# One request for the second tile of x, x laid out by tiles, and ten warm-up products in a two-layer kernel on TensorE

## The reference

```python
selected_W = W[cat_ids]
x = x + einsum('bsd,bdh->bsh', x, selected_W) + selected_b[:, None, :]
h = relu(einsum('bsd,bdf->bsf', x, wi[type_label]))
eo = einsum('bsf,bfd->bsd', h, wo[type_label])
s0, s1 = relu(x @ swi[0]) @ swo[0], relu(x @ swi[1]) @ swo[1]
gate_in = concatenate([eo[:, 0], s0[:, 0], s1[:, 0]], axis=-1)
w = softmax(relu(gate_in @ g1) @ g2, axis=-1)
x = x + eo * w[:, 0] + s0 * w[:, 1] + s1 * w[:, 2]
```

## Time and profile before

| | |
|---|---|
| median of 3 runs | 268.65 us (268.18 to 268.87) |
| the profiled execution, its own time | 268.71 us |
| its span, first to last instruction | 266.8 us |
| PE busy | 262.8 us, 99% of the span |
| DVE, ACT, POOL busy | 162.8, 150.0, 162.2 us |
| read and written in HBM | 16.00 and 2.10 MB |

### The profile page before, as it was taken

The page is one execution under the profiler, slowest core; times in us unless marked ns, Lnnn a source line. Parts: engine busy times, 40 slices in busy tenths (PEclk is TensorE's granted clock), DMA queues, the critical chain, the costliest instruction groups (busy, mean ns, idle before and its releaser), DMA issues.

```text
span 266.8 us, 3464 instructions
## 1 busy us (share of the span) xinstructions
PE 262.8 (99%) x1162; PEld 218.5 (82%) x1162; DVE 162.8 (61%) x246; ACT 150.0 (56%) x267; POOL 162.2 (61%) x171
## 2 busy tenths in 40 slices
PE   8999999999999999999999999999999999999995
PEld 8888888888888888888888888888888888888884
DVE  4679968635645434654445575345476577985664
ACT  3586457866575555665655644646545755645320
POOL 0269999999958949938944725625626528535000
PEclk9999999999999999999999999999999999999999
DMA  5654322012022012202022012012022022000404
GB/s 181 195 175 160 118 79 80 18 64 80 7 74 79 12 68 79 60 22 79 0 79 81 21 57 81 8 72 80 2 79 79 0 81 77 2 0 0 160 1 157
DMA packets 7473, 18.31 MB, mean 69 GB/s; under 512 B 1312, under 2 KB 2080, under 8 KB 7456
## 3 DMA queue, kind: packets, MB, share of 16 engines
q1 hardware_dynamic: 6880, 17.18, 19.4%
q10 hardware_dynamic: 576, 0.92, 1.0%
HBM read 16.00 MB, written 2.10 MB: 68 GB/s over the span
## 4 chain that ended last, share of the span: by engine, by line
PE 99%; DVE 0%; issue 0%; DVEq 0%
PE acc L755 48%; PE chain L755 23%; PE right L755 12%; PE left L755 6%; PE acc L764 4%; PE left L944 2%; PE left L810 1%; PE corner L755 1%; PE right L810 1%; PE corner L810 1%; PE chain L810 1%; DVE x L746 0%; DVE ones L641 0%; DVEq L745 0%
## 5 line engine op out<-in xcount | busy, mean ns | idle before, releaser
L296 POOL TENSOR_TENSOR m_lo<-staged,m_hi 128x512 fp32r<-128x512 f32 (+2 forms) x49 | 82.9, 1703 | 76.7 <-ACT m_hi L378 62.7
L755 PE MATMUL acc<-h_hi,m_hi 128*128 128x512 f32 x190 | 73.9, 389 | 0.0
L755 PE MATMUL acc<-h_lo,m_hi 128*128 128x512 f32 x190 | 73.9, 389 | 0.0
L755 PE MATMUL acc<-h_hi,m_lo 128*128 128x512 f32 x190 | 73.9, 389 | 0.0
L402 ACT COPY kept<-chain 128x512 f32<-128x512 f32 x66 | 38.9, 589 | 53.5 <-PE chain L755 53.5
L755 PEld LDWEIGHTS acc<-h_hi,m_lo 128*128 128x128 f32 x190 | 35.7, 188 | 7.4
L755 PEld LDWEIGHTS acc<-h_lo,m_hi 128*128 128x128 f32 x190 | 35.7, 188 | 7.4
L755 PEld LDWEIGHTS acc<-h_hi,m_hi 128*128 128x128 f32 x190 | 35.7, 188 | 7.3
L534 DVE SCALAR_TENSOR_TENSOR h_lo<-left,h_hi 128x512 fp32r<-128x512 f32 x24 | 16.6, 691 | 28.5 <-ACT h_hi L414 28.5
L296 POOL TENSOR_TENSOR staged<-staged 128x128 f32<-128x128 f32 x66 | 31.0, 484 | 1.7
L539 DVE TENSOR_TENSOR left<-left,kept 128x512 f32<-128x512 f32 x22 | 15.3, 695 | 23.9 <-PE left L755 23.9
(11 more groups left out here) (151 smaller groups left out, 441.7 us busy)
## 6 DMA issues: line engine op xcount, KB each, us to landing
staged<-mlp_w SPq DMA_DIRECT2D x22, 512.0 KB, 3.3
x<-x_t SPq DMA_DIRECT2D x5, 256.0 KB, 5.1
staged<-mlp_w SPq DMA_DIRECT2D x4, 256.0 KB, 3.3
out_t<-x SPq DMA_DIRECT2D x2, 512.0 KB, 3.3
x<-x_t ACTq DMA_DIRECT2D x3, 256.0 KB, 3.4
g_sb<-g SPq DMA_DIRECT2D x1, 768.0 KB, 3.8
out_t<-x SPq DMA_DIRECT2D x3, 256.0 KB, 2.3
w_raw<-cat_w SPq DMA_DIRECT2D x4, 128.0 KB, 2.3
```

What stands on the lines that cost most here:

```text
L296: return nc.gpsimd.tensor_tensor(out, a, b, ALU.subtract)
L755: last = nc.tensor.matmul(out[:, columns], half[:, slot, at:at + P], moving[:, columns], start=(start and n == 0), stop=(stop and n == 2), ...
```

## The change

Three things are changed. On the host, x is laid out by tiles: for each partition first both halves d of tile 0 (4 KB in one piece), then both halves of tile 1. The second tile of the first batch element is fetched by a single request of 128 rows of 4 KB, issued by ACT, in place of one request by SP and one by ACT; ACT issues it once `w_requested` is raised, in place of once part (0,0,0) has landed, and the semaphore `tile_loaded` stands for both parts. The second group of warm-up products has six in place of seven, so there are ten.

```diff
-WARMUP = (4, 7)
+WARMUP = (4, 6)
...
+        tile_loaded = sem("tile_loaded")
...
         def load_x(eng, b, t, d):
-            eng.dma_start(x1_part(b, t, d), x_t[b][:, d, t * TOK:(t + 1) * TOK]).then_inc(x_loaded[b][t][d], 16)
+            eng.dma_start(x1_part(b, t, d), x_t[b][:, t, d, :]).then_inc(x_loaded[b][t][d], 16)
...
-                if b == 0:
-
-                    load_x(sp, 0, 1, 0)
                 sp.dma_start(bias[:, b, :], cat_b[bass.ds(cat, 1)].rearrange("a p d -> p (a d)")).then_inc(bias_loaded[b], 16)
...
-                        sp.wait_ge(x_loaded[0][1][DC - 1], 16)
+                        sp.wait_ge(tile_loaded, 16)
...
             def x_hi_of(b, t, d):
-                act.wait_ge(x_loaded[b][t][d], 16)
+                act.wait_ge(tile_loaded if (b, t) == (0, 1) else x_loaded[b][t][d], 16)
...
-            act.wait_ge(x_loaded[0][0][0], 16)
-            load_x(act, 0, 1, 1)
+            act.wait_ge(w_requested, 1)
+            act.dma_start(x1[:, 0, 1, :, :], x_t[0][:, 1, :, :]).then_inc(tile_loaded, 16)
...
-        "x_t": np.asarray(x).reshape(B, S, DC, P).transpose(0, 3, 2, 1),
+        "x_t": np.asarray(x).reshape(B, S // TOK, TOK, DC, P).transpose(0, 4, 1, 3, 2),
```

More of the change, by code:

```diff
@@ L47, in build @@
 def build(nc, x_t, cat_w, cat_b, mlp_w, ids, g1, g2, out_t):
-    B, _, _, S = x_t.shape
+    B, _, HALVES, _, _ = x_t.shape
     D = DC * P
-    HALVES = S // TOK
     BANKS = mlp_w.shape[0]
```

## The result

The changed kernel takes 269.75 us (median of 8 runs, 269.27 to 270.70) against 268.39 us (8 runs, 268.18 to 268.87): a ratio of 1.0046, 95% interval 1.0036 to 1.0057. By the ratio it is slower by 1.2 us (the medians differ by 1.4), where 0.2 us less was forecast, and it lies above the forecast range of 268.0 to 269.1. The profiled execution took 269.88 us with a span of 268.0, so 1.2 us more than the profiled one of before, and it can be accounted for in full.

What follows compares the result with a forecast made beforehand. PE, busy 99% of the span, was taken as the bound. Span 266.8 less 0.2 for the warm-up product, plus 1.9 around the span, less 0.06 for the median, gave 268.45 us; range 268.0 to 269.1.

Steps and rivals of the forecast that it cites:

- What bounds the kernel: Whole span: PE, busy for 99% of it, bounds the kernel and never stands still after 1.06 us.
- One warm-up product less, -0.2 us: Before layer 0: PE starts 0.43 us earlier, less 0.20 for one more product at half speed; 0.2 us gain taken.
- When the request goes out, 3.1 us: ACT's request of the second tile: issued at 3.1 us, once ACT's table activation ends at 3.13.
- The price of the overlap, 0.1 us with a bound of 1.2: Weights' first half beside the tile's transfer: 0.1 us of delay, lower bound 0, upper bound 1.2 us.
- The prediction's own sign of being wrong: Weights in the changed profile: the prediction is wrong if they land over 1 us late.
- The tile's landing, 7.6 us: Second tile of x: lands at about 7.6 us, bounds 6.4 and 8.4; costs nothing at 7.6, 0.2 us at 8.4.
- The layout, 0: Fetching parts of x in 2 KB rows at another stride: 0 us, either way.
- C: Rival, weights over 0.1 us late: 0.4 us of delay gives 268.6 us, the 1.2 us bound 269.35; chance 0.16.
- E: Slower rival, PE idles before its first real product and full speed comes later: 270.0 to 271.4 us; chance 0.10.
- F: Faster rival, array's full speed comes ahead of the first real product: 1.0 us won, 267.65 us; chance 0.06.
- the clock's moment: PE's array early in layer 0: goes from half to full speed at 7.24 us, the same moment as before.

Runs made afterwards that it cites:

- e2: The kernel before with six in place of seven warm-up products in the second group and nothing else: 268.61 us, ratio 1.0008.
- e3: The changed kernel with ACT's tile request held until SP has issued both halves of the weights: 268.50 us, ratio 1.0003.
- e4: The changed kernel with ACT's single tile request gated as before, by the landing of part (0,0,0): 268.90 us, ratio 1.0006.
- e7: The changed kernel with the tile's single request issued by SP, behind the weights in SP's own queue: 268.70 us, ratio 1.0006.
- e1: The kernel before with x laid out by tiles and nothing else changed: 268.72 us, ratio 1.0004.
- e6: The changed kernel with seven warm-up products in the second group again: 269.56 us, ratio 1.0037.
- e14: e10 with seven warm-up products in the second group: 269.08 us, ratio 1.0020.
- e8: The kernel before, old layout, with the second tile in one early request by ACT (256 rows of 2 KB, gated by `w_requested`): 268.59 us, ratio 1.0001.
- e13: e8 with six in place of seven warm-up products in the second group: 268.46 us, ratio 0.9996.
- e9: The changed kernel with the tile requested at once behind the first tile, without the wait for `w_requested`, ahead of both weight halves: 270.66 us, ratio 1.0071.
- e11: e3 with the first tile, too, in one request of 4 KB rows: 270.37 us, ratio 1.0063.
- e12: e3 with four warm-up products in the second group: 268.62 us, ratio 1.0012.
- e5: The changed kernel with the tile in two requests of 2 KB rows, both by ACT at the same early gate: 269.06 us, ratio 1.0018.
- e10: The changed kernel with each row of x in memory padded by 64 elements, so the tile's request has 256 rows of 2 KB: 269.10 us, ratio 1.0016.

## Why the prediction was wrong

**What bounds the kernel.** Right, but not read to its end. PE never waited before, yet an operand was nearly late: the second tile's cast ended at 8.27 + 0.62 = 8.89 for a load at 9.06. e2 shows what follows: PE may come earlier only until it stands before the tile.

**One warm-up product less, -0.2 us.** The start did come 0.39 us earlier in e2, but the gain is nil, since the tile's landing takes it back. The slack of 0.17 us at that place stood in the rows. In e2, e3, e4 and e7 the 24 products end 3.7 us after the tile's first cast starts (8.47, 8.06, 8.90 and 8.26, against 12.18, 11.77, 12.61 and 11.96). With its cast at 8.27 the kernel before could end them at 11.98 at best, an estimate from these traces: 0.2 us were to be won there, whatever the warm-up and the clock do.

**When the request goes out, 3.1 us.** Wrong: 2.82. ACT issued it as soon as `w_requested` was raised, while the table was being loaded. The 0.3 us put it ahead of the weights' second half, requested at 2.98; behind it, at 3.41 and 3.40, it cost nothing (e3, e7).

**The price of the overlap, 0.1 us with a bound of 1.2.** This is the step that failed. I priced the first half of the weights alone, since it gates the first product, and gave the second half no line of its own, for it had 1.8 us and more to spare. Its cast started 3.1 us later (8.46, against 5.37 in the trace of before), PE waited 0.76 us for it, and product 7 began 1.08 us late. That is nearly the whole 1.19; the rest is a slower pair behind the gap. e3, with the order of the two requests turned round, shows it: no loss. The prediction's own sign of being wrong, weights over 1 us late, came true for the half that it hadn't priced. The first half, too, was cast 0.75 us later in this trace (5.70 against 4.95), but that isn't shown to be the tile's doing: it was 0.42 and 0.62 us late in e1 and e4 (5.37 and 5.57), where the tile is requested only behind both halves.

**The tile's landing, 7.6 us.** It landed at 8.1, near the bound of 8.4. Asked for earlier, it wasn't there much earlier: 8.06 in e3 with a request at 3.41. It scatters, too: in e6, with the changed kernel's requests, it was there at 7.6.

**The layout, 0.** Right by itself (e1). Together with the early request it isn't: 4 KB rows cost 1.0037 (e6), padded 2 KB rows 1.0020 (e14, of which 0.3 us, 0.0011, lies at the end of the kernel), rows of the old layout 1.0001 and 0.9996 (e8, e13).

**The rivals.** C had the right mechanism for the wrong half, and a size too small: 1.2 us at most, against 3.1. The Trainium skill (DMA: Bandwidth & Descriptors, Queues, rings and completion order) lets the engines take turns between the queues, a packet at a time. The trace agrees from 6.0 to 7.0 us, where both queues move; from 5.25 to 5.75 us q1 moved 2 packets beside q10's 32, and whether it had work then no row shows. E did not come in the changed kernel, in whose profile the distances double up to some 7.2 us as before; it is seen in the profiles of e9, e11 and e12.

F's condition, the rise ahead of the first real product, did come in e7, e13 and e14, though not its gain. By the distances of the matmuls PE was at full speed from 4.2 us on in e13's profile, 5.2 in e7's, 5.7 in e14's, 6.7 in those of e2 and e4, 7.0 in e6's and 7.2 in the two that the prediction is about, with the first matmul at 1.06 in all of them. In e13 it came in the warm-up, six of whose matmuls then fit into 0.83 us:

```profile
4.23 0.83 PE L942 MATMUL left<-ones 128*128 128x128 f32 x6
5.33 0.69 PE L762 MATMUL acc<-x_hi,w_hi 128*128 128x512 f32 x2 [0.27 <-ACT w_hi L431]
...
7.52 0.70 PE L762 MATMUL acc<-x_hi,w_hi 128*128 128x512 f32 x2 [0.59 <-ACT w_hi L388]
```

What the clock gives, PE then spends waiting: 0.59 us for the second half here, 0.42 us for the tile in e7. F's 1.0 us was not to be had as long as the tile lands near 8. The sum had the clock's moment as a fixed 7.2; that it matched in the changed kernel's profile is luck.

**How late may the second half be?** In five profiles (e13, e14, e5, e6, the changed kernel) the cast of the second half starts at 6.97, 7.14, 7.59, 7.93 and 8.46, and the 24 products end at 11.87, 12.04, 12.48, 12.85 and 13.36, each 4.9 us later. Before, they ended at 12.17. So by these traces a cast that starts up to about 7.3 costs nothing, and each microsecond beyond costs a whole one. (In e10's profile the first half, cast at 7.17, decides; e9 and e11 lose their time ahead of the second half, by the first half and by the index.)

What stays open: how the queues hold the second half back. The times show that a tile requested ahead of it in one request of 4 KB rows costs about 1 us or more (the changed kernel, e6, e9), and in one request of 2 KB rows about nothing in layer 0 (e8, e13, e14); yet in two requests of 2 KB rows, one ahead and one behind, it costs 0.5 us (e5). The experiments show that it is so and not where the data queue up. Each landing time is from one profiled execution, and these scatter: in the changed kernel's own trace the first half came 0.75 us later than before, in e6's with the same requests 0.3 us.

## What to carry to other kernels

When a large transfer is moved ahead, list everything issued within the next microsecond behind it, on either queue, and give each its own time of need; the one with the most slack is the one that is forgotten. Before costing an earlier start of the bounding engine, find the next operand it would run into: here it had 0.17 us to win, whatever the warm-up. And a small read on which a request depends (an index) is a transfer like the others: look at its time too when large transfers are moved. Before a single trace is read as the effect of a change, see where its full speed began: that moved by 3 us between the kernels' profiles here.

## What the runs showed of the hardware

- A request by ACT went out at 2.82 us, 0.02 us after the semaphore that it waits for was raised, while ACT's table was still being loaded (1.64 to 2.92): the table load and the activation that stand before it in the program did not hold it.
- With 512 KB in rows of 4 KB requested 0.16 us ahead on the other queue, 128 KB took 5.46 us from request to landing, in place of 2.4 to 2.6. With the same bytes in rows of 2 KB it took 3.95 us (e13).
- A read of an index took 1.71 us in place of 0.51 when the first tile was asked for in one request of 4 KB rows (e11), and 1.96 in place of 0.85 in one execution with rows of 2 KB (e8).
- Full speed came anywhere from 4.2 to 7.2 us in profiles in which PE didn't stop for more than 0.4 us before it. With stops of 1.0 to 1.3 us before it, it came at 9.4 to 10.3 us (e9, e11, e12), with one of 0.8 us at some 8.1 (e8), but after a stop of 1.5 us it was there at once (e10). In the changed kernel it came before the stop of 0.76 us and stayed. The Trainium skill (TensorE: Matmul & The Clock Gate, Part 1: The HAM clock gate) says that the chip's windows run freely, so that the moment depends on where in them the first matmul lands; the traces agree in that the moment varies with the first matmul always at 1.06.
